# Causal attention, a second attention and routed experts in one kernel: values two steps behind the scores, projections in halves, other places for the side work, and diagonal key tiles first in each causal run

## The reference, cut to what matters

```python
x = L0_attn_x                                            # (1, 2048, 128)
x = _layernorm(x + attn_ref(x, wq, wk, wv, wo))          # 16 heads, rope, causal
x = _layernorm(x + ffn_ref(x, ...))
# attn_ref: softmax(mask(q @ k.T / sqrt(8))) @ v, then @ wo.T
# ffn_ref:
x = x + _msa(_layernorm(x, ln1_w, ln1_b), w_qkv, w_proj) # 16 heads, over all 2048 rows
z = _layernorm(x, ln2_w, ln2_b)
one_hot = jax.nn.one_hot(jnp.argmax(z @ gate_w + gate_b, axis=-1), 8)
h = jax.nn.gelu(jnp.einsum('td,edh->teh', z, w1), approximate=True)
x = x + jnp.einsum('te,ted->td', one_hot, jnp.einsum('teh,ehd->ted', h, w2))
```

## Time and profile before

| | us |
|---|---|
| median of 3 runs | 946.25 |
| the runs | 947.0, 936.71, 946.25 |
| the profiled execution | 942.67 |
| its span, first to last instruction | 940.8 |
| mean granted clock of TensorE | 0.946 of 2.4 GHz |

### The profile page before, as it was taken

How to read it: one execution, slowest core, us unless ns; L and a number is a source line. 1 busy time by engine, 2 the same in 40 slices (tenths; PEclk the granted TensorE clock), 3 DMA queues, 4 the chain that set the end, 5 groups by cost and what they waited for, 6 DMA issues and landing times.

```text
span 940.8 us, 23853 instructions
## 1 busy us (share of the span) xinstructions
PE 828.4 (88%) x9744; PEld 366.6 (39%) x9744; DVE 323.9 (34%) x945; ACT 779.0 (83%) x913; POOL 221.1 (24%) x359
## 2 busy tenths in 40 slices
PE   5699898999999999999999999999999999992361
PEld 2344344444443344343444444443444434442130
DVE  3713625311521015210052332453331643325642
ACT  1568698899999999999999989999989999890630
POOL 4741121111110010000022432133322133331351
PEclk9789899999999999999999999999999999997575
DMA  7976220202020433700100001110001010000100
GB/s 258 268 224 175 82 56 1 91 2 46 18 74 1 103 79 90 226 1 2 46 8 24 1 2 43 33 40 2 2 2 30 5 38 2 2 13 17 39 13 28
DMA packets 34355, 51.58 MB, mean 55 GB/s; under 512 B 4032, under 2 KB 14656, under 8 KB 34240
## 3 DMA queue, kind: packets, MB, share of 16 engines
q1 hardware_dynamic: 32704, 46.30, 17.2%
q0 software_dynamic: 1536, 3.67, 1.3%
HBM read 29.12 MB, written 20.84 MB: 53 GB/s over the span
## 4 chain that ended last, share of the span: by engine, by line
PE 75%; DVE 9%; ACT 8%; issue 4%; DMA 2%; POOL 1%; POOLq 0%; SPq 0%; ACTq 0%; DVEq 0%
PE ps L476 70%; ACT probs L856 5%; PE ps L481 3%; PE ps L731 2%; ACT squares_blockdiag L893 1%; DVE ln_stats L1068 1%; DMA y_sorted<-early_late 1%; DVE ln_newton L1063 1%; DVE ln_newton L1061 1%; DMA z_rows<-y_sorted,slot_numbers 1%; POOL z_rows L1018 1%; DVE squares_blockdiag L1342 1%; DVE ln_newton L1062 0%; DVE z_rows L1077 0%; DMA early_late<-in_sin 0%
## 5 line engine op out<-in xcount | busy, mean ns | idle before, releaser
L856 ACT ACTIVATE probs<-ps 128x1024 f32<-128x1024 f32 (+3 forms) x832 | 735.2, 1014 | 66.4 <-PE ps L476 64.8
L476 PE MATMUL ps<-probs,values 128*9 128x256 f32 (+1 forms) x6528 | 430.2, 376 | 1.6 <-DVE q_rotated L1200 1.6
L476 PE MATMUL ps<-query_rows,key_rows 32*128 32x512 f32 (+3 forms) x1664 | 294.3, 487 | 21.6 <-ACT probs L856 18.5
L476 PEld LDWEIGHTS ps<-probs,values 128*9 128x9 f32 x6528 | 143.7, 90 | 185.2 <-issue 87.1
L476 PEld LDWEIGHTS ps<-query_rows,key_rows 32*128 32x128 f32 x1664 | 122.7, 184 | 220.0 <-ACT probs L856 112.2
L966 POOL TENSOR_SCALAR_AFFINE_SELECT probs<-probs 128x256 f32<-128x256 f32 x128 | 52.7, 418 | 242.7 <-ACT probs L856 239.6
L1005 POOL COPY parts<-early_late 128x512 f32 x63 | 37.1, 629 | 140.8 <-PE ps L476 140.8
L1200 DVE COPY q_rotated<-ps 128x512 f32<-128x512 f32 x30 | 20.7, 690 | 135.6 <-PE ps L476 135.6
L971 POOL DMA_INDIRECT z_sorted<-z_rows,slot_numbers x16 | 15.8, 989 | 214.4 <-DVE slot_numbers L1330 211.5
L998 POOL COPY parts<-parts 128x512 f32 x72 | 47.9, 707 | 43.4 <-PE ps L476 32.0
L1212 DVE RECIPROCAL recip<-ps 128x16 f32<-128x16 f32 x32 | 8.2, 256 | 90.7 <-PE ps L481 90.7
(11 more groups left out here) (169 smaller groups left out, 560.4 us busy)
## 6 DMA issues: line engine op xcount, KB each, us to landing
k_scratch<-parts SPq DMA_DIRECT2D x16, 512.0 KB, 3.8
q_scratch<-parts SPq DMA_DIRECT2D x16, 512.0 KB, 5.2
query_rows<-q_scratch SPq DMA_DIRECT2D x32, 256.0 KB, 4.9
key_rows<-k_scratch SPq DMA_DIRECT2D x20, 256.0 KB, 4.7
key_rows<-k_scratch SPq DMA_DIRECT2D x16, 192.0 KB, 4.4
parts<-in_w SPq DMA_DIRECT2D x1, 2048.0 KB, 8.3
early_late<-in_w SPq DMA_DIRECT2D x8, 256.0 KB, 7.1
early_late<-z_sorted SPq DMA_DIRECT2D x4, 384.0 KB, 3.1
```

Of the source, the lines that this page charges most:

```text
L476: return nc.tensor.matmul(out, l, r, start=start, stop=stop, skip_group_check=True)
L856: nc.scalar.activation(Pr[:, t % KEPT, 2 * p:2 * p + 2, lo:BLK], score_banks(t, p)[:, :, lo:BLK], ACT.Exp, bias=-SHIFT[r["a"]], scale=SCAL ...
```

## The change

Five things change.

- In `run`, after the scores of step n the two halves of step n-2 follow, both together. Before, it was the second half of n-2 and the first of n-1 (none to three halves at the first steps of a run).
- In `run_step`, a causal run begins with its four diagonal tiles and then takes the older tiles; GpSimd's cuts follow that order.
- `m_up` and `m_down` are issued in two halves: one at the position before their place, the other at it. An up half is 256 of 512 columns; a down half two of four chunks. The waits stand ahead of the first half, the semaphore behind the second.
- Places: the rounds' `up` 25, 31, 38, 44, 50, 57 (from 26, 32, ..., 56), `turn` 29, 36, 42, 48, 54, 61 and `down` 33, 40, 46, 53, 59, 63; tanh one step after `up` rather than two; the sorted rows at 22 and 23 rather than 24 and 25; `post_project` at 6 rather than 7; some of the preparation one step to two steps later; the first bound's matmul at 5 rather than 1.
- GpSimd sends row block 1 ahead of the first four weight copies, block 2 between these and the next four, block 3 behind them, with no wait for step 19.

```diff
-UP_AT = (26, 32, 38, 44, 50, 56)
-SORTED_AT = (24, 25)
-TANH_AT = {at + 2: r for r, at in enumerate(UP_AT)}
+UP_AT = (25, 31, 38, 44, 50, 57)
+TURN_AT = (29, 36, 42, 48, 54, 61)
+DOWN_AT = (33, 40, 46, 53, 59, 63)
+SORTED_AT = (22, 23)
+TANH_AT = {at + 1: r for r, at in enumerate(UP_AT)}
...
-    (13, 14, 15, 17, 20, 21, (22, 24, 26, 28)),
-    (13, 17, 19, 21, 23, 25, (28, 32, 36, 40)),
+    (14, 16, 18, 20, 22, 23, (24, 26, 28, 30)),
+    (14, 17, 19, 21, 23, 25, (28, 32, 36, 40)),
     (14, 17, 20, 22, 24, 26, (28, 32, 36, 40)),
-    (13, 14, 16, 18, 20, 22, (25, 26, 29, 30)),
+    (13, 15, 17, 18, 20, 22, (25, 26, 29, 30)),
 )
-BOUND1_AT, OK1_AT = 1, 9
+BOUND1_AT, OK1_AT = 5, 9
...
             causal, kt = r["a"] == 1, r["k0"] + n
+            if causal:
+                kt = (r["qb"] * TB + n) % r["k1"]
...
-                        cut=2 * (done + kt % TB) + 1 if cut else None, start=n == 0, stop=kt == r["k1"] - 1)
+                        cut=2 * (done + kt % TB) + 1 if cut else None, start=n == 0, stop=n == r["k1"] - r["k0"] - 1)
...
-            def m_up(b, k, r):
-
-                pe.wait_ge(m_w1, 4 * (b * ROUNDS + r + 1))
-                side_free(b, k, ("sorted", 1))
-                for g in range(4):
-                    last = mm(ps[g * TS:(g + 1) * TS, side_bank(b, k), :], slots(4 * r + g), w1_of(b, r)[g])
-                last.then_inc(m_side, 1)
+            def m_up(b, k, r, halves=(0, 1)):
+
+                if 0 in halves:
+                    pe.wait_ge(m_w1, 4 * (b * ROUNDS + r + 1))
+                    side_free(b, k, ("sorted", 1))
+                for n in halves:
+                    c = slice(n * HID // 2, (n + 1) * HID // 2)
+                    for g in range(4):
+                        last = mm(ps[g * TS:(g + 1) * TS, side_bank(b, k), c], slots(4 * r + g), w1_of(b, r)[g][:, c])
+                if 1 in halves:
+                    last.then_inc(m_side, 1)
...
-                for c in range(TB):
+                for c in (c for n in halves for c in (2 * n, 2 * n + 1)):
...
-                    if n == 0 and old:
-                        values(old[-2], 1)
-                        values(old[-1], 0)
-                    elif n == 1 and old:
-                        values(old[-1], 1)
-                    elif n == 2:
-                        values(mine[0], 0)
-                    if n >= 2:
-                        values(mine[n - 2], 1)
-                        values(mine[n - 1], 0)
+                    if n >= 2 or old:
+                        behind = mine[n - 2] if n >= 2 else old[n - 2]
+                        values(behind, 0)
+                        values(behind, 1)
...
-                todo = {5: [lambda: post_turn(n - 1)], 7: [lambda: post_project(n - 1)]}
+                todo = {5: [lambda: post_turn(n - 1)], 6: [lambda: post_project(n - 1)]}
...
-                        todo[at] = [lambda k=k, name=name, r=r: side_op[name](b, k, r)]
+                        if name in ("up", "down"):
+                            todo[at - 1] = [lambda k=k, name=name, r=r: side_op[name](b, k, r, (0,))]
+                            todo[at] = [lambda k=k, name=name, r=r: side_op[name](b, k, r, (1,))]
+                        else:
+                            todo[at] = [lambda k=k, name=name, r=r: side_op[name](b, k, r)]
...
                     if b < NB - 1:
-                        if r:
+                        if r == 0:
+                            row_out(b, 1)
+                        else:
                             pool.wait_ge(m_side, issued(b, "up", r - 1))
                         for g, e in enumerate(mine):
                             nc.gpsimd.tensor_copy(w1s[g], W1[:, bass.ds(e * HID, HID)]).then_inc(m_w1, 1)
                         if r == 0:
-                            row_out(b, 1)
+                            row_out(b, 2)
...
                     if r == 0 and b < NB - 1:
-                        row_out(b, 2)
-                        pace(first_step(2, b + 1) + 19)
                         row_out(b, 3)
```

More of the change, by code:

```diff
@@ L115, in first_step, with side_order @@
     return runs_in(a, qb)[0]["t0"] if qb < NB else RUNS[-1]["t0"] + S // P if a == 2 else first_step(2, 0)
-def side_order(at, turn, down):
-    ops = [(at[r], "up", r) for r in range(ROUNDS)]
-    ops += [(at[r] + turn, "turn", r) for r in range(ROUNDS)]
-    ops += [(at[r] + down, "down", r) for r in range(ROUNDS)]
+def side_order(up, turn, down):
+    ops = [(at, name, r) for name, places in (("up", up), ("turn", turn), ("down", down)) for r, at in enumerate(places)]
     return [(SORTED_AT[n], "sorted", n) for n in range(2)] + sorted(ops)
-IN_SHADE = side_order(UP_AT, 5, 7)
-AT_END = side_order(tuple(30 + 6 * r for r in range(ROUNDS)), 8, 13)
+IN_SHADE = side_order(UP_AT, TURN_AT, DOWN_AT)
+AT_END = side_order(*(range(first, first + 6 * ROUNDS, 6) for first in (30, 38, 43)))
 OPS = len(IN_SHADE)
@@ L833, in _ @@
                         mine = run(r, side, freed, mine)
-            values(mine[-2], 1)
+            for p in range(2):
+                values(mine[-2], p)
             values(mine[-1], 0)
@@ L1034, in _ @@
                     for i in range(TB):
-                        cut(run_step(r, qb * TB + i))
+                        cut(run_step(r, i))
             for b in range(NB):
```

9 lines of the change are left out of this document (5 added, 4 removed).

## The result

| | before | after |
|---|---|---|
| median of 12 runs, us | 943.24 | 937.38 |
| lowest and highest | 936.71, 947.0 | 932.93, 947.68 |
| the profiled execution | 942.67 | 936.19 |
| its span | 940.8 | 934.4 |

The ratio is 0.9943, 95% interval 0.9916 to 0.997. The same kernel measured again on another chip gave 0.9978 (0.9951 to 1.0006). Two of the twelve runs after, 947.13 and 947.68 us at a mean clock of 0.933 and 0.931, were slow ones and are left out of the ratio. So the change wins between nothing and 0.8%, which is within 1% of no change; the forecast of 944 was 7 us too long, inside its range of 930 to 957. Its sum for the profiled execution was +1.9 us, and the two spans differ by -6.4.

The account below looks back on a forecast made before the run. The prediction took some 80 us of ScalarE waiting for TensorE as all that could be won. Its terms summed to +1.9 us on the profiled 942.67, so 944.6, stated as 944 us, range 930 to 957.

Parts of the forecast that it names:

- Diagonal first: Causal run starts: gaps of 0.46 and 1.49 us, 0.7 to 0.8 more than now per run; +9.0 us over 12 runs.
- The branch: Causal blocks: the branch at step 3 of the last run, hidden now, shows three times, +1.7 us.
- B: Rival, faster: the diagonal costs nothing extra, since TensorE runs ahead over short steps, and no clock falls; 930.5 us, chance 0.27.
- Sorted rows at 22: Routed blocks: TensorE waits for the sorted rows' load, 2.6 us in the first stage and 2.3 in the others, +7.2 us.
- The term of 3.4: Routed blocks: TensorE's clock halves after the wait for sorted rows in two of three stages, +3.4 us, bounds 0 and 5.1.
- Rounds: Routed blocks: projections in halves at new places win a net 4.0 us per stage, 12.0 in all; bounds 1.5 and 6.5.
- the early tanh: Routed rounds: the tanh one step earlier finds its argument up to 0.15 us late, costing 0.5 us a stage.
- Output projection at 6: TensorE's 1.45 us idle at step 10 for the layernorm goes, -3.6 us; back to back with the turn costs +0.9.
- Preparation and bound check: Causal blocks: moved preparation -3.5 and -4.3 us, uncovered side work +3.5; first block's check +1.6, shorter values -1.2.
- C: Rival, slower: weight copies come a whole step (1.8 us) late at three up halves per stage; 957.9 us, chance 0.15.
- D: Rival, does nothing: rounds bound by TensorE's columns, halves cost twice 0.47 us, stalls trade places; 943 to 947 us, chance 0.13.
- A: The forecast itself: routed gains are given back at the sorted rows and causal run starts; 938 to 951 us, chance 0.45.

Follow-up runs that it names:

- experiment 1: The changed kernel with each causal run's diagonal tiles last again: 937.38 us, ratio 0.9912 to the kernel before.
- experiment 7: The changed kernel with row blocks 2 and 3 sent after the second and fourth weight copy and diagonal tiles last: 925.69 us, ratio 0.9816 to before.
- experiment 4: The changed kernel with the values one step behind again: 942.88 us, ratio 0.9976 to the kernel before.
- after again: The changed kernel, unedited, measured once more on another chip: 940.34 us, ratio 0.9978 to the kernel before.
- experiment 9: The kernel of experiment 8 with the tanh of round 0 two steps after its up projection rather than one: 923.71 us, ratio 0.9767 to before.
- experiment 10: The kernel of experiment 9 with the first bound's matmul at 1 rather than 5: 922.95 us, ratio 0.9756 to the kernel before.
- experiment 2: The kernel before with one edit, diagonal tiles first in each causal run: 946.85 us, ratio 1.0055 to the kernel before.
- experiment 3: The changed kernel with whole up and down projections, each at the later of its two positions: 952.14 us, ratio 1.0095 to the kernel before.
- experiment 8: The kernel of experiment 7 measured again on a third chip, as yardstick: 928.9 us, ratio 0.9804 to the kernel before.
- experiment 5: The changed kernel with all four row blocks sent ahead of the weight copies: 945.13 us, ratio 1.0000 to the kernel before.
- experiment 11: The kernel of experiment 8 with the values one step behind again: 932.87 us, ratio 0.985 to the kernel before.
- experiment 6: The changed kernel again, 940.34 us (ratio 0.9978 to before), and with row blocks 2 and 3 after the second and fourth weight copy, 937.49 us (0.9933).

## Why the prediction was right, and where it was off

**Diagonal first: right in the mechanism, and in the sum partly by luck.** 0.46 and 1.49 us over ScalarE's floor, ahead of steps 3 and 4 of a run, were worked out; in causal block 3 of after they are 0.9 and 1.5. The last two runs of that block, which have hardly any side work, are 28.8 and 28.9 us long, and both 27.8 with the diagonal last (experiment 1), so that the order costs 1.0 there rather than 0.75; in the first two, with the side work, it costs 0.5 and 0.7. The branch, taken at 1.7 us in all, hardly shows: it follows step 3 of the fourth run, which is 0.1 longer than the third. In its place stand the 2 us of the clock in block 1, which the sum did not have. So the 10.7 us, 10.9 in the profiles and 11.8 in time (experiments 1, 7), are made up otherwise than forecast. The rival that two steps of distance would let TensorE run over the short steps (B) is refuted by the gaps, and experiment 4 adds that the one ahead of step 4 is larger with two steps than with one. That the short exponentials then meet the predecessor's full values and the turn is the working of the prediction; no run takes it apart further.

**Sorted rows at 22: right.** Forecast 2.6, 2.3 and 2.3 us, measured 2.66, 2.50 and 2.50. The clock, of which two falls in three were taken, fell in none of these stages in after's profiled execution, in two in that of after again. The term of 3.4 is a matter of the execution; it is two fifths of the 8.4 us by which the profiled one (936.19) was shorter than the sum (944.6). The span of after again is 937.2, only 3.6 under before's.

**Rounds: right in the mechanism, mis-sized.** The routed blocks won 12.3 us together. Without the sorted rows (+7.7), the layernorm at step 10 (-3.6), step 6 (+0.4) and the early tanh (+1.9) that is 12.3 + 7.7 - 3.6 + 0.4 + 1.9 = 18.7, or 6.2 a stage, where the prediction took 4.0 out of bounds of 1.5 and 6.5. (The 3.6 and 0.4 are the prediction's own, not measured apart.) A round of six steps takes 11.6 to 11.7 us, from one tanh to the next, near the 11.5 forecast. The two costs that it set against the gain failed: the up halves at 43 and 49 wait for no weights, and that at 56 in the first block alone, 0.39 us (577.14), rather than 0.3 to 0.4 three times a stage; and the tanh costs its own 0.52 in rounds 1 to 5 and nothing more.

**The tanh of round 0: missed.** The prediction gave 0.5 a stage to arguments that come 0.15 late. What comes late is one of six, by 0.5: VectorE makes it beside GpSimd's weight copies. The row for it, here of after, has its like in the trace of before, where a spare step hid it:

```profile
642.98 3.20 POOL L1008 COPY parts<-parts 128x512 f32 x4 [10.81 <-PE ps L479]
643.64 1.05 DVE L1349 TENSOR_TENSOR squares_blockdiag<-early_late 128x512 f32<-128x512 f32 x1
644.73 0.98 DVE L1350 SCALAR_TENSOR_TENSOR squares_blockdiag<-squares_blockdiag,early_late 128x512 f32<-128x512 f32 x1
647.34 0.50 PE L479 MATMUL ps<-query_rows,key_rows 32*128 32x512 f32 x2 [1.04 <-ACT probs L864]
...
655.79 0.69 DVE L1349 TENSOR_TENSOR squares_blockdiag<-q_work 128x512 f32<-128x512 f32 x1
```

The operation of round 0 takes 1.05, that of round 1, with GpSimd idle, 0.69. When a deadline moves a step closer, each operation before it wants looking up in its slowest form, not its mean. Experiment 9 shows the price with the clock's part in it: 3.5 us by the ratios, where 1.9 were worked out from the wait alone.

**Output projection at 6: right.** No idle time of 1.45 stands at step 10.

**Preparation and bound check: right within 1 us.** In causal block 1 the idle time ahead of z's turn is 1.56 (forecast 1.6), and the check at step 5 holds the values up for 1.77. The row names GpSimd's cut as what ended that wait, but VectorE's copy of the sums, behind the check, ended only 0.1 us before that cut did (56.27 and 56.38), and with the check moved (experiment 10) the wait is gone:

```profile
102.41 0.93 PE L484 MATMUL ps<-ident,z_rows 128*128 128x128 f32 x4 [1.56 <-DVE z_rows L1249]
103.50:107.00 3.50, 3.50 (x39) 1.10 (x40) 0.69 (x1) 2.44 (x3) 0.00 (x0) 0.64 0.02 5
...
56.42 1.90 PE L479 MATMUL ps<-probs,values 128*9 128x256 f32 x16 [1.77 <-POOL probs L974]
```

The clock fell behind the 1.56 as well (0.64 over the stretch behind it); the prediction had counted that fall as gone. With the diagonal last it is gone, and there the terms can be seen by themselves: experiment 1's blocks 1, 2 and 3 are 1.1 and 3.8 us shorter and 1.0 longer than before's, where the prediction's terms without the diagonal give -1.2, -3.7 and +0.6. But the -4.3 of block 2 is not the moved preparation's alone: experiment 2, with the preparation at its old place and the diagonal first, lost the idle time of that block too. The term for the check (+1.6) is there; taking it back (experiment 10) made the first block 2.6 us shorter and the time no shorter that could be told, with falls in the next two blocks of that profile.

**Rivals.** C (weights a whole step late at three up halves) is refuted by the one wait of 0.39. D (projections cost the same in halves) is refuted by experiment 3. B's other half, no fall of the clock, did occur in the profiled execution, in the routed blocks. That the median came out at 937 and not at 944 lies mostly in the rounds, mis-sized by 6.7 us, and, in the profiled execution, in falls that did not come; A's picture, gains given back at the sorted rows and at the causal run starts, holds.

## What to carry to other kernels

Where one engine sets the pace and another is just inside it, splitting a side operation of 0.9 us over two steps is worth trying first (7 to 9 us here, over 36 such operations). Work that is started early must be followed to the transfer that feeds it: the sorted rows' transposes, moved two steps forward, met 2.5 to 2.7 us of waiting. Where irregular tiles (the short diagonal ones) stand in a run is worth as much (11 us here): at the end of a run they cost a single gap of 0.55, at its start two, of 0.56 and 1.35. And before moving several things together, look at what each does alone: undoing one of the five parts and correcting two others by a step or two made a gain of 0.2 to 0.6% into one of 2.3%. And a single profile of each kernel can mislead: by the falls and late updates of its execution a part of the kernel that no edit touched was up to 8 us longer.

## What the runs showed of the hardware

**The clock.** Idle times of TensorE of 2.66 and 2.50 us left the granted clock at 1.00 (2.4 GHz) in after's profiled execution; in another execution of the same kernel it fell to 0.50 (1.2 GHz) for 3.4 us behind the same waits of the first two blocks (2.78 and 2.61) and not behind that of the third (2.48); and in the yardstick of experiment 8 it fell behind a wait of 1.03. So the length of the wait before it alone does not decide. The prediction's reading, that it stays up behind 1.45 and falls behind 2.38, was drawn from two cases and is refuted. In most kernels here the executions follow their mean granted clock: for after 0.959 went with 932.93 to 933.87 us, 0.951 and 0.952 with 936.0 to 936.4, and 0.940 with 941.02. In experiment 9, where the wait at position 26 is gone, they don't: 922.58 and 926.07 us both at 0.949, 923.57 at 0.957. A fall cost ScalarE 1.1 and 1.6 us in experiment 8, and some 1.4 in a routed block of after again.

**A late update.** With four scattering transfers of GpSimd sent back to back (494.31 to 496.85 and the one at 492.88), the semaphore updates behind TensorE's scores came up to 2.9 us after the scores' end in the first routed block, and 3.1 in the other two; with weight copies between the transfers none did there. A lateness of 0.6 to 1.7 us was seen near the starts of the second and third routed block in experiments 1, 3, 4 and 5 and 8 to 11, and none there in before, after, or experiments 2, 6 and 7. That is each profile of the first and of the third chip, and none of the second. It costs about 1 us a block: the second one of experiment 8 is 2.2 longer than that of experiment 7, and its fall accounts for 1.1. In experiment 9 it is what is left of the idle times over 1 us beside the sorted rows: 1.29 of TensorE at 711.44, four steps into the third routed block. Since 7 and 8 are one kernel, it depends on the chip or the execution, and by these profiles rather on the chip. Which resource the update waits for is open.

**VectorE beside GpSimd.** Beside GpSimd's copies an operation of VectorE with both inputs in SBUF takes longer, and even a tiny one can last as long as several of them. Timeline of after:

```profile
628.75 1.72 POOL L1015 COPY parts<-early_late 128x512 f32 x3
628.76 1.73 DVE L1070 TENSOR_TENSOR ln_newton<-ln_newton 128x4 f32<-128x4 f32 x1
631.27 0.16 DVE L1070 TENSOR_TENSOR ln_newton<-ln_newton 128x4 f32<-128x4 f32 x1
```

The same operation of 128x4 takes 0.16 with GpSimd idle and 1.73, the length of three copies, beside them. The Trainium skill (SBUF — State Buffer, section "SBUF: two separate sides") says that VectorE and GpSimd share a port pair as an exclusive lock, held for a whole instruction, and that a VectorE operation with two SBUF inputs needs it against a GpSimd operation that reads SBUF, as these copies do. The trace agrees in kind; that one operation lasts through three copies in a row, rather than to the end of the one that is running, is more than that section states.
